# A new order of work in a unit of a scan over sixteen images, its five small products read in 32-row groups, and TensorE's walk unrolled

## The reference

```
x_dbl = einsum('bkdl,kcd->bkcl', xs, x_proj_w);  dtr, Bs, Cs = split(x_dbl, [8, 24])
dts = softplus(einsum('bkrl,kdr->bkdl', dtr, dt_w) + dt_b)          # d = 256 channels
h = exp(dt_l * A) * h + (dt_l * x_l) * b_l ;  y = sum_n h * c_l      # n = 16 states
```

## Time and profile before

| | before |
|---|---|
| median of three runs | 17334.62 us |
| the profiled execution, whole | 17319.04 us |
| its span, first to last instruction | 17316.8 us |
| mean granted TensorE clock, as a share of full speed | 0.823 |
| PE busy | 13233.5 us (76%) |
| DVE busy | 11342.2 us (65%) |
| ACT busy | 9996.2 us (58%) |
| POOL busy | 5298.9 us (31%) |

### The profile page before, as it was taken

How to read it: one execution, slowest core, us unless ns; L and a number is a source line. 1 busy time by engine, 2 the same in 40 slices (tenths; PEclk the granted TensorE clock), 3 DMA queues, 4 the chain that set the end, 5 groups by cost and what they waited for, 6 DMA issues and landing times.

```text
span 17316.8 us, 195473 instructions
## 1 busy us (share of the span) xinstructions
PE 13233.5 (76%) x48256; PEld 7576.2 (44%) x48256; DVE 11342.2 (65%) x15030; ACT 9996.2 (58%) x22003; POOL 5298.9 (31%) x4760
## 2 busy tenths in 40 slices
PE   5778778787787877878777787877878777787766
PEld 4444444444444344443444444444443444434422
DVE  3584775847668485774857758476584856848575
ACT  1375664747657475674756647466574755747533
POOL 6441431414224042341413314143240422404100
PEclk7878888797887978878788887888879788797867
DMA  5442332423234142332323323232242323414100
GB/s 163 114 115 76 98 95 79 115 72 103 80 94 115 60 115 70 104 110 64 115 71 103 102 73 115 79 96 87 86 116 64 110 73 101 116 59 115 57 7 12
DMA packets 661942, 1557.08 MB, mean 90 GB/s; under 512 B 76952, under 2 KB 347484, under 8 KB 650588
## 3 DMA queue, kind: packets, MB, share of 16 engines
q0 software_dynamic: 368640, 1208.25, 24.3%
q1 hardware_dynamic: 290012, 302.96, 5.8%
q10 hardware_dynamic: 2304, 33.56, 0.5%
HBM read 1338.32 MB, written 206.14 MB: 89 GB/s over the span
## 4 chain that ended last, share of the span: by engine, by line
PE 62%; ACT 16%; issue 8%; DVE 6%; ACTq 4%; POOL 2%; DMA 1%; DVEq 1%; SPq 0%; POOLq 0%
PE psum L1098 12%; PE psum L1108 9%; ACT arena L446 9%; PE psum L1289 6%; PE psum L1164 6%; PE psum L1194 5%; PE psum L1298 4%; PE psum L1199 3%; PE psum L1211 3%; PE psum L1117 2%; ACTq L459 2%; PE psum L1068 2%; ACT arena L457 2%; ACT arena L460 2%; POOL arena L700 2%
## 5 line engine op out<-in xcount | busy, mean ns | idle before, releaser
L650 POOL DMA_INDIRECT gathered<-cell_table,index_now x2880 | 3179.3, 1104 | 4137.7 <-PE psum L1098 1941.8
L1098 PE MATMUL psum<-pack,arena 128*128 128x128 f32 x6912 | 1530.9, 407 | 2487.5 <-ACT arena L446 2245.9
L1098 PEld LDWEIGHTS psum<-pack,arena 128*128 128x128 f32 x6912 | 1325.9, 216 | 2882.1 <-issue 2881.4
L650 POOL DMA_INDIRECT arena<-cell_table,index_now x1440 | 1628.9, 1131 | 2333.3 <-PE psum L1098 2031.2
L1108 PEld LDWEIGHTS psum<-samples_t,pack 128*128 128x128 f32 x9216 | 1628.6, 275 | 642.5 <-issue 621.5
L446 ACT ACTIVATE gathered<-gathered,weight_now 128x128 f32<-128x128 f32 x5760 | 1735.4, 388 | 27.9 <-issue 27.9
L1108 PE MATMUL psum<-samples_t,pack 128*128 128x128 f32 x9216 | 1733.2, 367 | 15.2 <-ACT samples_t L433 15.2
L446 ACT ACTIVATE arena<-arena,weight_now 128x128 f32<-128x128 f32 x5760 | 1734.2, 390 | 0.0
L433 ACT COPY samples_t<-psum 128x384 f32<-128x384 f32 x1536 | 725.3, 472 | 1733.3 <-PE psum L1098 1502.5
L1098 PE MATMUL psum<-pack,gathered 128*128 128x128 f32 x11520 | 1545.3, 287 | 59.7 <-DVE gathered L829 59.7
L1194 PE MATMUL psum<-arena,pack 64*128 (+1 forms) x1024 | 937.1, 1012 | 663.1 <-issue 478.3
(11 more groups left out here) (165 smaller groups left out, 20934.0 us busy)
## 6 DMA issues: line engine op xcount, KB each, us to landing
cell_table<-arena SPq DMA_DIRECT2D x64, 2112.5 KB
gathered<-cell_table,index_now POOLq DMA_INDIRECT x2880, 3.6
arena<-in_x SPq DMA_DIRECT2D x16, 2048.0 KB, 7.7
image<-in_x SPq DMA_DIRECT2D x16, 2048.0 KB, 8.3
x_dram<-image SPq DMA_DIRECT2D x16, 2048.0 KB, 10.3
arena<-x_dram SPq DMA_DIRECT2D x16, 2048.0 KB, 8.6
out<-arena ACTq DMA_DIRECT2D x16, 2048.0 KB, 7.2
arena<-cell_table,index_now POOLq DMA_INDIRECT x1728, 3.7
```

What stands on the lines that cost most here:

```text
L650: pool.indirect_dma_start(gathered[m][:, n * CORNERS * C:(n + 1) * CORNERS * C], None, table, bass.IndirectOffsetOnAxis(ap=index_now[:, pa ...
L1098: last = pe.matmul(psum[:, T_BANK + m % 2, n * TILE:(n + 1) * TILE], corners[:, (n * CORNERS + q) * C:(n * CORNERS + q + 1) * C], ident, s ...
```

## The change

Three things are changed together.

1. **Order in a unit.** TensorE: both spreads first, then both halves of the next unit's step sizes, then `turn` 2 *of the tile before*, `convolve` of that tile, `turn` 0 and `turn` 1 of this one, the product with `fast_rows`, and the flag. ScalarE: `evacuate` 2 of the tile before, decays, `weigh` 1, `soft` of both halves in one piece (its Exp and Ln run over both halves at once), `evacuate` 0, `weigh` 2, `evacuate` 1, branch. VectorE: `weigh` 0 and the next tile's indices go from the unit's start to a place behind the flag, `add_tile` behind the product with B. `turn` alternates PSUM banks by `(par + m) % 2`, so that two are always in use.
2. **32-row groups.** `proj_b` now holds the step rows of all directions twice, in rows 0 to 31 and 32 to 63, and B in rows 64 to 127; `proj_c` holds C twice. `dtw` has 64 rows. The five small products read 32 rows each: step sizes of half 0 rows 0 to 31 and of half 1 rows 32 to 63, `spread_b` and the product with `fast_rows` rows 64 to 95 (k = 0, 1) or 96 to 127 (k = 2, 3), `spread_c` rows 0 to 31 or 32 to 63.
3. **Unrolled walk.** TensorE writes out all 32 unit bodies instead of looping over pairs; the other engines keep `walk`.

TensorE, the start of a unit with a tile, before: two products of the scan (L1194 `spread_b`, L1199 `spread_c`), with the convolution (L1108) and `turn` 0 (L1098, `gathered`) between them.

The diff, cut to its core (VectorE's and ScalarE's unit bodies are moved as the text above says):

```diff
+        def walk_unrolled(unit):
+            for n in range(UNITS):
+                k, c = divmod(n, PARTS)
+                unit(k, c, c % 2, divmod(n + 1, PARTS) if n + 1 < UNITS else None)
...
-    psum[:, T_BANK + m % 2, ...]
+    psum[:, T_BANK + (par + m) % 2, ...]
-                pe.wait_ge(S["t_used"], group - (m > 0) + SEED["t_used"])     # seed 1
+                pe.wait_ge(S["t_used"], group - 1 + SEED["t_used"])           # seed 2
...
 step_sizes:
-    pe.matmul(psum[:, Z_BANK + j, :], dtw[:, k * DI + j * C:k * DI + (j + 1) * C], part_of(proj_b, k, c), ...)
+    pe.matmul(psum[:, Z_BANK + j, :], dtw[j * QUAD:(j + 1) * QUAD, k * C:(k + 1) * C],
+              part_of(proj_b[j * QUAD:(j + 1) * QUAD, :], k, c), ...)
...
 TensorE's unit_of:
+                    low, high = [slice(at + k // 2 * QUAD, at + (k // 2 + 1) * QUAD) for at in (0, PC)]
                     spread_b(0, 0)                       # now rows `high`
+                    spread_c(0, 0)                       # now rows `low`
+                    if after:
+                        step_sizes(b, *after)
                     if with_next:
                         if not is_(t, 0):
+                            turn(b + 1, t - 1, 1 - par, 2)
                             convolve(b + 1, t - 1)
                         turn(b + 1, t, par, 0)
-                    spread_c(0, 0)
+                        turn(b + 1, t, par, 1)
...
                     (product with fast_rows, now rows `high`; flag)
-                    if with_next:
-                        turn(b + 1, t, par, 1)
-                    if after:
-                        step_sizes(b, *after, [1])
-                    if with_next:
-                        turn(b + 1, t, par, 2)
                     (read the flag, branch)
```

More of the change, by code:

```diff
@@ L522, in unit_of @@
                     t = k * PARTS + c
-                    if with_next and 1 in BY_ACT:
-                        weigh(b + 1, t, par, 1)
+                    if with_next and not is_(t, 0):
+                        evacuate(b + 1, t - 1, 1 - par, 2)
                     def decays(step, n, j):
@@ L536, in unit_of @@
                     if with_next:
[L537 removed]
+                        weigh(b + 1, t, par, 1)
                     if after:
[L539 removed]
+                        soft(b, *after, 1 - par)
                     if with_next:
[L541 removed]
+                        evacuate(b + 1, t, par, 0)
                         weigh(b + 1, t, par, 2)
[L543 to L544 removed]
+                        evacuate(b + 1, t, par, 1)
                     act.wait_ge(S["flag_set"], unit + 1)
@@ L553, in unit_of @@
                                 decays(n, bass.ds(n, 1), j)
-                    if with_next:
-                        evacuate(b + 1, t, 2)
                 exp_and_log()
-                for j in range(2):
-                    soft(b, 0, 0, 0, j)
+                soft(b, 0, 0, 0)
                 walk(act, unit_of)
+                if with_next:
+                    evacuate(b + 1, TILES - 1, 1, 2)
                 for s in range(CH + 1):
@@ L897, in unit_of @@
                     v.drain()
+                    v.tensor_mul(fast[:, :], least[:, :], decay_max[:, 2 * k:2 * k + 2])
+                    v.tensor_mul(local2(u2, k), local2(r2, k), part2_of(inner_x, k, c))
+                    v.drain()
+                    v.tensor_scalar(fast[:, :], fast[:, :], EXACT_ZERO, None, ALU.is_lt).then_inc(S["flag_in"], 1)
+                    if with_next:
+                        weigh(b + 1, t, par, 0)
                     if with_next and after:
@@ L904, in unit_of @@
                         weights(t + 1, 1 - par)
[L905 to L913, removed]
                     def scans(step, n):
@@ L920, in scans @@
                         v.tensor_mul(linear2(l2), in_scan_order2(u2, k), in_scan_order2(spread(B_BANK), k)).then_inc(S["b_used"], 1)
+                        if first and with_next and not is_(t, 0):
+                            add_tile(b + 1, t - 1)
                         v.drain()
@@ L1179, in layer1 @@
                     for j in range(2):
-                        last = pe.matmul(psum[0:PC, 2 + q % 2, :], wt("proj_c")[:, j * PC:(j + 1) * PC], piece(inner_x[:, j, :], q), start=j == 0, stop=j == 1)
+                        last = pe.matmul(psum[:, 2 + q % 2, :], wt("proj_c")[:, j * 2 * PC:(j + 1) * 2 * PC], piece(inner_x[:, j, :], q), start=j == 0, stop=j == 1)
                     last.then_inc(S["pc_done"], 1)
@@ L1246, in layer1 @@
                     own_wait(pe)
+                    turn(b + 1, TILES - 1, 1, 2)
                     convolve(b + 1, TILES - 1)
```

73 lines of the change are left out of this document (35 added, 38 removed).

## The result

The changed kernel takes 16626.96 us (median of four runs, 16625.41 to 16637.47) against 17337.85 before: 0.9593 of the time, 95% interval 0.9577 to 0.9610. That is 711 us less; 16860 was forecast, with 16710 as the range's lower end.

What follows compares the result with a forecast made beforehand. A ring over TensorE and ScalarE, 20.35 us a unit, was taken as the bound, VectorE's floor 6% below. 17319 - 592 of VectorE's waits + 120 left = 16847; the median lies 16 above, so 16860 us; range 16710 to 17290.

Steps and rivals of the forecast that it cites:

- A ring over TensorE and ScalarE: In units with a tile, a chain of waits from one `turn` 2 to the next, 20.35 us, bounds the old kernel.
- All of VectorE's waits: VectorE's waits for convolution and softplus in units, 39.5 us an image, 592 in all, can go; 120 stay.
- The floor: VectorE's own work in a unit without waits: 18.34 us in direction 0, 19.94 in directions 1 and 3, unchanged by reordering.
- rival 4: VectorE's unexplained gap ahead of L829, 23.4 us an image, shrinks and ring A never shows: 16720 us, chance 0.07.
- ring A: New order's chain over TensorE, from scan products through `turn` 2 to VectorE's branch: 16.6 to 18.8 us with overlap, 17.7 taken.
- The price of the products: TensorE's four scan products, overlapping, take 5.5 half products' time: 2.9 us at full clock, 5.1 at half.
- Rival 1: TensorE's scan products do not overlap, ring A is 17.9 to 21.1 us, 430 us come back: 17170 us, chance 0.19.
- Rival 2: TensorE's clock stays at 1.2 GHz and nothing overlaps: 17690 us, or 18690 if later steps are cold too; chance 0.13.
- Unrolling at nothing: TensorE's unrolled walk gains at most 1.05 us a unit, in a hidden place; nothing was taken for it.
- The last image unchanged: The last image's units are VectorE's alone, 470 of 530 us busy; a change over 10 us would refute the forecast.
- The rest of an image unchanged: The part of an image outside its tile-carrying units, 32% of the time, changes by nothing that could be found.
- Units of 18.3 to 18.6 and 20.0 us: Sign of a right forecast: units take these times by turns of direction.

Runs made afterwards that it cites:

- indices_early: The changed kernel with VectorE's wait for and copy of the next tile's indices and weights put back behind the least step, ahead of the flag's product: 16781.82 us (0.9689).
- serial_products: The changed kernel with added TensorE waits, so that spread_c and both step sizes each start only after the product before has ended: 18370.59 us (1.0602 of before).
- old_order_rows: The kernel before, in its old order, with TensorE's walk unrolled and the 32-row products with their layout: 16775.78 us (0.9672 of before).

## Why the prediction was wrong

- *A ring over TensorE and ScalarE is the bound, and VectorE's own work a floor a few per cent below it:* right. The old kernel did not move by 0.1% with a faster VectorE, and the changed one did.
- *All of VectorE's waits, 592 us, can go, 120 will stay:* 472 was the sum, and 485 went in the whole run (516 by the fifth image). Right within 10%.
- *The floor:* this step failed. "The unit stays 18.34 long, since that only changes place" took VectorE's unit, gaps included, from the earlier trace rows. Its gaps depend on the order too: 34.6 us an image at the moved places became 21.2, which is 201 us in all by this image and 187 in the whole run. `indices_early` shows a part of them by itself (155 us). The earlier trace rows showed the largest of them (23.4), and rival 4 named it with a chance of 0.07, but gave it almost nothing: its 16720 is 140 below the forecast, of which 120 is ring A never showing and only some 20 the gap. With the 187 in the sum the forecast would have been 16673, below the stated range as the result is.
- *The price of the products:* the way was right, the size was not. 2.9 us at full clock and 5.1 at half were taken; 2.2 and 4.0 it was. The assumed rule, that `spread_c` and half 0 collide in rows 0 to 31 in directions 0 and 1, shows in the start of half 0 (0.5 us after `spread_c`, 0.26 in directions 2 and 3) but not in the time of the four, 4.0 at half clock with the collision and without. Neither 6 nor 5 half products came out but about 4; why it is 4 in both, no run shows. The statement of the Trainium skill, "TensorE: Matmul & The Clock Gate", Part 3, that products in different row groups run concurrently holds here for float32 too, at 7.5 / 4.0 = 1.9 times for four products in three groups, below the 3.07 that it states for four tiles. The drain at a change of tiling mode, which the Trainium skill states in "TensorEngine Tiling (Array Packing)", Key Properties, can't be told apart in these rows: `turn` 2, which reads all 128 rows, starts at 4877.56 in the half-clock unit above, where the four products end at 4877.63.
- *Rival 1 (17170 without overlap):* its mechanism is what the new order without row groups shows (VectorE waits for the flag), at 16930. The ring cost less than taken: the clock was higher (0.81 in the units), and in its fifth image the four products of one unit take 3.9 us (4917.10 to 4920.97), those of another 6.9 (4971.14 to 4978.03).
- *Rival 2 (slower):* did not occur, though the granted clock in the units fell from 0.76 to 0.70. `serial_products`, with slower products and a clock of 0.66, shows that products this slow do make the new order slower than the old kernel.
- *Unrolling at nothing:* right in the new order (4 us, inside the noise), wrong in the old (123), where TensorE's branch lies in the ring. TensorE's idle time ahead of `spread_b` with no releaser fell there from 478.3 to 402.9 us in the whole run, which is 75 of the 123; the rest stays open.
- *The last image unchanged:* right. *The rest of an image unchanged:* right in the sum, by luck. Outside the units' stretches the changed kernel takes 7207 us against 7219, but the new order with the loop takes 46 more there (7265), and the row groups take 75 off. *Units of 18.3 to 18.6 and 20.0 us:* the fifth image has means of 18.1, 19.8, 18.4 and 20.1 for the four directions, so direction 0 lies below its range: that is the floor again. *`spread_c` half a product after `spread_b`:* it starts after 0.25 us, less than a quarter of a product's 1.12.

## What to carry to other kernels

Where a ring over several engines is the bound, the floor set by the next engine is neither its busy time nor the length of one old unit without waits: its gaps without a releaser count as well, and they move with the order of its instructions. List them in the profile before the ring is cut, and put them in the sum. On the engine that will be the bound, do first what others wait for, try short copies behind a long instruction where they have a gap of their own, and expect something from unrolling a loop only where its engine is the bound or in the ring. If an experiment adds waits to undo an overlap, price the waits themselves before reading its size.

## What the runs showed of the hardware that was not expected

- Two float32 products of 32 rows and 512 columns in different row groups run fully beside each other (1.13 us for both, one alone 1.12 in the same kernel, `old_order_rows`). One that reads the same rows as the product before it starts 0.5 us after it, where one in other rows starts after 0.25.
- A semaphore wait of TensorE for its own last product costs 0.40 us on top of that product's end (617 us in 1518 such waits of `serial_products`, 0.41 each).
- In the new order the granted clock of the units is lower with 32 rows than with 64 to 128 (0.70 against 0.81), and the kernel is still faster; in the old order the rows hardly move it (0.74 against 0.75). In the last image it fell from 0.55 to 0.50 with TensorE busy for 129 us instead of 285. Whether the rows or the shorter busy time bring it down, no run separates.
